# Order of one copy and one maximum on VectorE in the cross-attentions of a Perceiver block

## The chip, the core and the metric

The kernel runs on one core of a Trainium2 chip. What counts is the device time of one execution in microseconds; several runs are given by their median. Five engines work side by side and meet only at semaphores: TensorE (PE in the profile, its weight loads PEld), VectorE (DVE), ScalarE (ACT), GpSimd (POOL) and SyncE (SP), which only issues transfers.

## What is computed

Sixteen items with 64 query rows of 256 features pass through two layers. Each layer opens with a cross-attention from the 64 rows (layer-normalized) to 1601 context rows, 16 heads of 16 features. The first one adds relative-position terms to scores and values, the second one takes a mask. Cut to what matters:

```python
def cross_attention(query, context, mask, Wq, bq, Wkv, bkv, Wout, bout, num_heads):
    q = query @ Wq + bq
    kv = context @ Wkv + bkv
    k, v = (kv[0], kv[1])
    scores = jnp.einsum('bhid,bhjd->bhij', q, k) * scale
    scores = jnp.where(mask[:, None, None, :], -jnp.inf, scores)
    attn = jax.nn.softmax(scores, axis=-1)
    out = jnp.einsum('bhij,bhjd->bhid', attn, v)
    return out @ Wout + bout
...
    x = x + _L0_xattn_ref(_layernorm(x, axis=-1), ctx_1024, ctx_1024, ...)
    x = x + _L0_attn_ref(...)
    x = x + _L0_ffn_ref(...)
    x = x + _L1_xattn_ref(_layernorm(x, axis=-1), ctx_1024, mask_BxS2_bf0, ...)
    x = x + _L1_attn_ref(...)
    x = x + _L1_ffn_ref(...)
```

## The kernel before

All six stages are one program. `cross_attention` is called twice: the relative-position one (its tiles are named x0_) fills about 60 to 890 us of the span, the masked one (x3_) about 1360 to 2020 us; the latent attention and the mixture of experts lie between, the delta rule and the last feed-forward behind.

**Steps.** A cross-attention walks over its 16 items. In one step it attends to item b and works ahead on item b + 1, for which it projects keys and finds the row maxima that the softmax needs. The 1601 context rows of an item are 13 chunks of 128 (the last has 65), taken in pairs, c = 0, 2, ..., 12. The maxima are found in 16 pieces (`maximum(u)`): TensorE multiplies bf16 keys and queries into two PSUM banks (L779, 400 or 401 columns each; in the first four pieces of the relative-position attention L784 adds the relative terms), and VectorE reduces both banks in one instruction into `mx` (L634). While a step attends there is one pair of banks for this, 5 and 6, so TensorE may write piece u only when VectorE has read piece u - 1 (`max_read`).

**The order on TensorE** within a pair c is written out by hand: scores of c (L831 and L839) into banks 1 to 4; the first piece, `SCORED[c]`; the value projection of the chunks c + 2 and c + 3 (L804) into bank 0; the second piece, `PROJECTED[c]`; probabilities times values of the chunks c - 2 and c - 1 (L821) into bank 7; the third piece, `VALUED[c]`. At c = 0 there is only the second piece. In this text S4 is a piece of SCORED with number 4, P5 one of PROJECTED, V6 one of VALUED; a pair from c = 2 to c = 10 has one of each, from S1, P2, V3 to S13, P14, V15.

**VectorE** keeps its own order, also by hand. Besides the three reductions it copies the projected values from bank 0 into the tile `V` (`values(c + 2)`, L652). That copy frees bank 0 for the next value projection, and it waits for two semaphores, that of the projection and, from c = 4 on, `av_done`, which tells that TensorE is through with the old values in the slots of `V`. ScalarE takes the exponentials of the scores (L527, L529) and the projected keys (L464).

A step with both parts, attending and working ahead, runs 15 times in each cross-attention, 30 times in all. The last step of each only attends and holds no maxima.

Of the kernel before, what the change touches and what calls it, by code (L numbers as in the profile page):

```python
# [179 lines left out]
def cross_attention(nc, g, n, m, ctx_t, w, coming, x=None, rel=None, mask=None):  # L180
# [5 lines left out]
    with nc.cleanup_on_exit(), ExitStack() as ctx:  # L186
# [142 lines left out]
        PROJECTED = {0: 0, 2: 2, 4: 5, 6: 8, 8: 11, 10: 14}  # L329
# [222 lines left out]
        def _(dve):  # L552
# [31 lines left out]
            def body(bank, plan, i, p, flags):  # L584
                ahead, attend, tail = flags
# [44 lines left out]
                def maximum(u):  # L630
                    kb, k = divmod(u, 4)
                    dve.wait_ge(max_full, UN * (b + 1) + u + 1)
                    first = 5 if attend else 1 + 2 * (u % 2)
                    dve.reduce_max(mx[:, H0[k]:H0[k] + 3:2, kb], g.PS[:, first:first + 2, 0:KBS[kb]], AXX).then_inc(max_read, 1)  # L634
# [11 lines left out]
                def values(c):  # L646
                    n2 = min(2, NCH - c)
                    pb, use = plan.V[c // 2]
                    dve.wait_ge(full[pb], bank.value(pb, use))
                    if later(b) or c >= 6:  # L650
                        dve.wait_ge(av_done, NCH * b + (c - 4 if c >= 6 else 0))
                    dve.tensor_copy(V[0:CHK[c], c % 6:c % 6 + n2, :, 0:HD],  # L652
                                    PJ[pb][0:CHK[c], 0:D * n2].rearrange("p (a h d) -> p a h d", a=n2, h=H)).then_inc(free[pb], 1)
# [6 lines left out]
                for c in range(0, NCH, 2) if attend else ():  # L660
                    if ahead and c in SCORED:
                        maximum(SCORED[c])
                    if c + 2 < NCH:
                        values(c + 2)
                    if ahead and c in PROJECTED:
                        maximum(PROJECTED[c])
                    if ahead and c in VALUED:
                        maximum(VALUED[c])
                if ahead:
# [15 lines left out]
                if tail and not attend:  # L685
# [4 lines left out]
                    ln_last_vector(dve, g, n + 1)  # L690

            run(dve, body)

        @block.tensor
# [2016 lines left out]
```

## Time and profile before

| | us |
|---|---|
| median of 3 runs | 2829.75 |
| lowest and highest run | 2828.48, 2829.79 |
| span of the profiled execution | 2820.9 |
| TensorE busy with matmuls in it | 2592.8 (92%) |
| TensorE busy with weight loads | 1855.1 (66%) |
| VectorE busy | 1386.3 (49%) |
| ScalarE busy | 1042.5 (37%) |
| GpSimd busy | 532.0 (19%) |

The span runs from the first to the last instruction of one execution. It is 8.85 us shorter than the median of the runs; the time of that very execution is not listed apart. Engines overlap, so the busy times do not add up. Because each engine works through its own list in order and waits only at semaphores, what matters is not which engine is busiest but, at each place, which wait ends last.

### The profile page before, as it was taken

Reading aid. Unit: us, or ns where it says so; the run is one execution under the profiler, and the core shown is the slowest. Engines: PE = TensorE matmul, PEld = TensorE weight load, DVE = VectorE, ACT = ScalarE, POOL = GpSimd, SP = SyncE. Lnnn points to the kernel's source line nnn. Section 1 sums busy time; section 2 is a strip of 40 time slices with the busy share of each in tenths; the row PEclk is TensorE's granted clock in tenths of the full one; section 3 lists DMA queues with packets and bytes.
Section 4 is the critical chain, followed back from the end, with each engine's and each line's share of the span. In section 5 each row is a group of like instructions: output and inputs, shape, how many; then the busy total and the mean of one; then the engine's idle time right before and its main releaser. Section 6 shows DMA issues by size and latency. Waiting matters only on the chain. (4 is left out here: it accounts for less than half of the span.)

```text
span 2820.9 us, 91874 instructions
## 1 busy us (share of the span) xinstructions
PE 2592.8 (92%) x42047; PEld 1855.1 (66%) x42047; DVE 1386.3 (49%) x2238; ACT 1042.5 (37%) x1400; POOL 532.0 (19%) x400
## 2 busy tenths in 40 slices
PE   7999999999999789998999999999979999988798
PEld 3666666666666556664666666666647777777466
DVE  4454544544544831115545455555465454554378
ACT  2333333333323421114444444444434445444223
POOL 2423424434324000002111111111011111111000
PEclk8999999999998579999999999999999999999899
DMA  2110110110100030101111111112010000000200
GB/s 90 32 43 25 37 37 25 37 37 27 42 20 2 1 121 30 45 20 44 43 33 41 34 40 37 37 37 68 3 51 3 3 3 3 4 3 4 79 1 16
DMA packets 49607, 88.88 MB, mean 32 GB/s; under 512 B 8544, under 2 KB 44224, under 8 KB 47952
## 3 DMA queue, kind: packets, MB, share of 16 engines
q1 hardware_dynamic: 49200, 83.08, 9.6%
q8 instruction: 331, 5.42, 0.8%
q14 instruction: 44, 0.36, 0.0%
q0 software_dynamic: 32, 0.02, 0.0%
HBM read 82.04 MB, written 1.05 MB: 29 GB/s over the span
## 5 line engine op out<-in xcount | busy, mean ns | idle before, releaser
L634 DVE TENSOR_REDUCE x_mx<-banks 128x2 f32<-128x800 f32 (+1 forms) x512 | 505.3, 990 | 162.4 <-PE banks L779 133.2
L804 PE MATMUL banks<-x_wv,x_cT 128*128 128x256 f32 (+1 forms) x1664 | 419.3, 394 | 12.3 <-DVE x_nmb L641 12.3
L709 PE MATMUL banks<-x_cT,x_wk 128*128 128x400 f32 (+1 forms) x1024 | 385.4, 519 | 9.3 <-DMA x_cT<-in_ctx 5.9
L804 PEld LDWEIGHTS banks<-x_wv,x_cT 128*128 128x128 f32 (+1 forms) x1664 | 296.4, 187 | 83.6 <-issue 24.5
L527 ACT ACTIVATE x_PT<-banks 128x2048 f32<-128x2048 f32 (+1 forms) x112 | 196.5, 1755 | 372.1 <-PE banks L839 372.1
L529 ACT ACTIVATE x_PT<-banks,x_kbs 128x1024 f32<-128x1024 f32 (+1 forms) x208 | 221.1, 1110 | 287.7 <-PE banks L839 287.7
L652 DVE COPY x_V<-banks 128x512 f32<-128x512 f32 (+1 forms) x224 | 146.2, 653 | 338.1 <-PE banks L804 337.7
L709 PEld LDWEIGHTS banks<-x_cT,x_wk 128*128 128x128 f32 x1024 | 189.5, 193 | 140.5 <-issue 26.8
L839 PE MATMUL banks<-x_qbd,x_kT 32*128 32x128 f32 x6656 | 248.6, 272 | 0.0
L839 PEld LDWEIGHTS banks<-x_qbd,x_kT 32*128 32x128 f32 x6656 | 244.0, 183 | 3.5
L821 PE MATMUL banks<-x_PT,x_V 128*32 128x64 f32 x13312 | 233.8, 221 | 3.8 <-issue 3.0
L821 PEld LDWEIGHTS banks<-x_PT,x_V 128*32 128x32 f32 x13312 | 196.7, 110 | 55.4 <-issue 47.5
L779 PE MATMUL banks<-x_kbf,x_qbf 32*128 32x400 bf16 (+1 forms) x1024 | 174.8, 339 | 53.5 <-DVE x_mx L634 44.9
L406 POOL TENSOR_TENSOR x_kbf<-x_kT,x_mb 128x802 bf16<-128x802 f32 (+1 forms) x64 | 110.2, 1725 | 597.4 <-ACT x_kT L464 597.4
L447 POOL TENSOR_TENSOR x_Ej<-x_PT,x_kmask 128x1024 f32<-128x1024 f32 x64 | 148.7, 2358 | 128.8 <-ACT x_PT L527 128.8
L779 PEld LDWEIGHTS banks<-x_kbf,x_qbf 32*128 32x128 bf16 x1024 | 49.7, 91 | 176.2 <-DVE x_mx L634 91.8
L2069 PE MATMUL banks<-d_KQ,d_KB 64*64 64x64 f32 x3584 | 129.3, 221 | 7.4 <-ACT d_KB L1743 3.5
L1415 DVE SCALAR_TENSOR_TENSOR X<-banks,e_comb,X 128x256 f32<-128x256 f32 x72 | 34.8, 484 | 205.5 <-PE banks L1453 205.5
L464 ACT ACTIVATE x_kT<-banks,x_bk 128x400 f32<-128x400 f32 (+1 forms) x128 | 76.0, 594 | 158.6 <-PE banks L709 158.6
L2069 PEld LDWEIGHTS banks<-d_KQ,d_KB 64*64 64x64 f32 x3584 | 117.1, 134 | 23.2 <-issue 23.0
L1440 PE MATMUL banks<-XNT,e_wu 128*128 128x512 f32 x288 | 128.6, 600 | 0.4 <-DVE e_pr L1366 0.4
L1453 PE MATMUL banks<-e_wd,e_hT 128*128 128x256 f32 x576 | 127.1, 379 | 0.0
(353 smaller groups left out, 3671.4 us busy)
## 6 DMA issues: line engine op xcount, KB each, us to landing
x_cT<-in_ctx SPq DMA_DIRECT2D x96, 400.0 KB, 3.6
x_cT<-in_ctx SPq DMA_DIRECT2D x32, 401.0 KB, 3.6
e_wu<-in_mo_up SPq DMA_DIRECT2D x9, 512.0 KB, 3.5
e_wd<-in_mo_down SPq DMA_DIRECT2D x9, 512.0 KB, 4.5
x_mrow<-in_mask_row SPq DMA_DIRECT2D x1, 3202.0 KB, 16.2
t_w<-in_db_w SPq DMA_DIRECT2D x3, 1024.0 KB, 7.2
d_wqk<-in_db_qk SPq DMA_DIRECT2D x1, 2048.0 KB, 7.9
t_wgu<-in_fp_gu SPq DMA_DIRECT2D x1, 1536.0 KB, 10.4
```

The lines of the kernel that those rows point to most:

```text
L447: pool.tensor_tensor(Ej[:, j, :].rearrange("p (h q) -> p h q", h=H), PT[:, 0, 0, :].rearrange("p (h q) -> p h q", h=H), kmask[:, j, None, ...
L527: act.activation(out, got, ACT.Exp, scale=HD ** -0.5, bias=0.0).then_inc(exp_done, n2)
L529: act.activation(out[:, :, a], got[:, :, a], ACT.Exp, scale=HD ** -0.5, bias=kbs[0:CHK[c], p, c + a:c + a + 1]).then_inc(exp_done, 1)
L634: dve.reduce_max(mx[:, H0[k]:H0[k] + 3:2, kb], g.PS[:, first:first + 2, 0:KBS[kb]], AXX).then_inc(max_read, 1)
L652: dve.tensor_copy(V[0:CHK[c], c % 6:c % 6 + n2, :, 0:HD], PJ[pb][0:CHK[c], 0:D * n2].rearrange("p (a h d) -> p a h d", a=n2, h=H)).then_in ...
L709: last = pe.matmul(PJ[pb][:, 0:KBS[k]], wk[:, c, gg, :], cT[:, (p + 1) % 2, c, KB0[k]:KB0[k] + KBS[k]], start=c == 0, stop=c == KC - 1)
L779: last = pe.matmul(g.P[first + x][:, 0:KBS[kb]], qbf[rows(r), gg, :, :].rearrange("p i q -> p (i q)"), kbf[rows(r), gg, keys], start=True, ...
L804: last = pe.matmul(PJ[pb][0:CHK[c + k], D * k:D * k + D], cT[:, p, cc, 128 * (c + k):128 * (c + k) + CHK[c + k]], wv[:, cc, :], start=cc = ...
L821: last = pe.matmul(OT[r:r + 32, S * (h // 4):S * (h // 4) + S], V[0:CHK[c], c % 6, h, :], PT[0:CHK[c], c // 2 % NPT, c % 2, S * h:S * h + ...
L839: last = pe.matmul(SC[r][0:CHK[c + a], at:at + HPT * S], kT[rows(r), p, gg, 128 * (c + a):128 * (c + a) + CHK[c + a]], qbd[rows(r), p, gg, ...
L1440: last = pe.matmul(g.P[f][:, :], wu[:, q, c, 128 * f:128 * f + 128], g.XNT[:, c, 512 * t:512 * t + 512], start=c == 0, stop=c == KC - 1)
L2069: last = pe.matmul(out, lhs(E[e], hp), rhs(E[e], hp), start=k > 0 or start, stop=True, skip_group_check=True)
```

## The change

In the steps that work ahead, VectorE runs the reduction of the second piece before the copy of the values that were projected in front of it, not after it. TensorE, ScalarE, GpSimd and SyncE keep every instruction and its place.

```diff
@@ -660,10 +660,10 @@
                 for c in range(0, NCH, 2) if attend else ():
                     if ahead and c in SCORED:
                         maximum(SCORED[c])
+                    if ahead and c in PROJECTED:
+                        maximum(PROJECTED[c])
                     if c + 2 < NCH:
                         values(c + 2)
-                    if ahead and c in PROJECTED:
-                        maximum(PROJECTED[c])
                     if ahead and c in VALUED:
                         maximum(VALUED[c])
```

VectorE's list at the start of the second step of the relative-position attention, before; the first of the two copies in the first row stands ahead of the pairs, L634 is a reduction, L652 a copy:

```order
L652 COPY x0_V<-banks 128x32x16 x2
L634 TENSOR_REDUCE x0_mx<-banks 128x2 x2
L652 COPY x0_V<-banks 128x32x16
L634 TENSOR_REDUCE x0_mx<-banks 128x2 x3
L652 COPY x0_V<-banks 128x32x16
L634 TENSOR_REDUCE x0_mx<-banks 128x2 x3
```

The same place in the changed kernel:

```order
L652 COPY x0_V<-banks 128x32x16
L634 TENSOR_REDUCE x0_mx<-banks 128x2
L652 COPY x0_V<-banks 128x32x16
L634 TENSOR_REDUCE x0_mx<-banks 128x2 x2
L652 COPY x0_V<-banks 128x32x16
L634 TENSOR_REDUCE x0_mx<-banks 128x2 x3
```

Each copy in the pairs has gone behind one reduction: before, three reductions in a row are P, V and the next S; now they are V, the next S and the next P.

The end of the same step on VectorE, before:

```order
L652 COPY x0_V<-banks 128x32x16
L634 TENSOR_REDUCE x0_mx<-banks 128x2 x3
L652 COPY x0_V<-banks 65x16x16
L634 TENSOR_REDUCE x0_mx<-banks 128x2 x2
L676 TENSOR_REDUCE x0_nm<-x0_mx 128x4x2
```

And in the changed kernel:

```order
L652 COPY x0_V<-banks 128x32x16
L634 TENSOR_REDUCE x0_mx<-banks 128x2 x3
L652 COPY x0_V<-banks 65x16x16
L634 TENSOR_REDUCE x0_mx<-banks 128x2
L676 TENSOR_REDUCE x0_nm<-x0_mx 128x4x2
```

The last copy (65 rows) stands between P14 and V15, no longer in front of P14.

TensorE's list beside it, the pairs c = 4 and c = 6 of that step's kind, the same in both kernels:

```order
L779 MATMUL banks<-x0_kbf,x0_qbf 128x400 x2
L804 MATMUL banks<-x0_wv,x0_cT 128x256 x4
L779 MATMUL banks<-x0_kbf,x0_qbf 128x400 x2
L821 MATMUL banks<-x0_PT,x0_V 32x64 x32
L779 MATMUL banks<-x0_kbf,x0_qbf 128x400 x2
L831 MATMUL banks<-x0_nmb,x0_ones 128x512 x4
L839 MATMUL banks<-x0_qbd,x0_kT 128x128 x16
L779 MATMUL banks<-x0_kbf,x0_qbf 128x400 x2
```

The rows of L779 are S, P, V and the next S; nothing has moved on this engine.

## Rows read from the trace of the kernel before

**Rows 1.** Waits of the whole span: engine, line, released by: us, times, longest us.

```profile
PEld banks L779 <- DVE x_mx L634: 91.8, 278, 0.6
```

**Rows 2.** Stretch of a masked step: PE, PEld, DVE, ACT, POOL busy; clock, DMA share, GB/s.

```profile
1559.00:1588.00 29.00, 27.03 (x657) 20.17 (x655) 19.48 (x23) 14.18 (x14) 0.00 (x0) 1.00 0.17 46
```

**Rows 3.** Timeline (start, duration, instruction, idle before), masked step, P5 to P8.

```profile
1569.16 0.34 PE L779 MATMUL banks<-x_kbf,x_qbf 32*128 32x400 bf16 x2
1569.27 0.69 DVE L652 COPY x_V<-banks 128x512 f32<-128x512 f32 x1 [0.93 <-PE banks L804]
...
1569.88 0.98 DVE L634 TENSOR_REDUCE x_mx<-banks 128x2 f32<-128x800 f32 x1
1570.91 0.09 PEld L779 LDWEIGHTS banks<-x_kbf,x_qbf 32*128 32x128 bf16 x2 [0.54 <-DVE x_mx L634]
...
1571.30 0.99 DVE L634 TENSOR_REDUCE x_mx<-banks 128x2 f32<-128x800 f32 x1 [0.44 <-PE banks L779]
1572.35 0.10 PEld L779 LDWEIGHTS banks<-x_kbf,x_qbf 32*128 32x128 bf16 x2 [0.17 <-DVE x_mx L634]
...
1572.62 1.59 PEld L804 LDWEIGHTS banks<-x_wv,x_cT 128*128 128x128 f32 x8 [0.18 <-issue]
...
1574.55 0.34 PE L779 MATMUL banks<-x_kbf,x_qbf 32*128 32x400 bf16 x2
```

**Rows 4.** Timeline, the same step earlier: P2, then S4.

```profile
1563.68 0.34 PE L779 MATMUL banks<-x_kbf,x_qbf 32*128 32x401 bf16 x2
...
1566.93 0.12 PEld L779 LDWEIGHTS banks<-x_kbf,x_qbf 32*128 32x128 bf16 x2 [0.24 <-issue]
```

**Rows 5.** Timeline, the same step later: P11, S13, then P14 and V15.

```profile
1579.93 0.34 PE L779 MATMUL banks<-x_kbf,x_qbf 32*128 32x400 bf16 x2
...
1583.20 0.09 PEld L779 LDWEIGHTS banks<-x_kbf,x_qbf 32*128 32x128 bf16 x2 [0.17 <-DVE x_mx L634]
...
1583.48 1.08 PE L804 MATMUL banks<-x_wv,x_cT 128*65 128x256 f32 x4
...
1584.60 0.42 DVE L652 COPY x_V<-banks 65x256 f32<-65x256 f32 x1
1584.64 0.34 PE L779 MATMUL banks<-x_kbf,x_qbf 32*128 32x400 bf16 x2
...
1585.03 0.99 DVE L634 TENSOR_REDUCE x_mx<-banks 128x2 f32<-128x800 f32 x1
1586.07 0.09 PEld L779 LDWEIGHTS banks<-x_kbf,x_qbf 32*128 32x128 bf16 x2 [0.22 <-DVE x_mx L634]
```

**Rows 6.** Timeline, first step: two reductions in a row, then one that waits for them.

```profile
60.52 1.89 DVE L634 TENSOR_REDUCE x_mx<-banks 128x2 f32<-128x800 f32 x2 [0.27 <-PE banks L779]
...
62.44 0.19 DVE L676 TENSOR_REDUCE x_nm<-x_mx 128x8 f32<-128x32 f32 x1
```

**Rows 7.** Timeline, relative-position step, pair c = 2: P2, V3, S4.

```profile
340.75 0.30 PE L784 MATMUL banks<-x_rmaskb,x_Dxb 128*128 128x66 bf16 x4
...
341.19 0.98 DVE L634 TENSOR_REDUCE x_mx<-banks 128x2 f32<-128x802 f32 x1
...
342.51 0.30 PE L784 MATMUL banks<-x_rmaskb,x_Dxb 128*128 128x66 bf16 x4
...
342.84 1.00 DVE L634 TENSOR_REDUCE x_mx<-banks 128x2 f32<-128x802 f32 x1 [0.67 <-PE banks L784]
343.95 0.12 PEld L779 LDWEIGHTS banks<-x_kbf,x_qbf 32*128 32x128 bf16 x2
```

**Rows 8.** Timeline, relative-position step, pair c = 0: P0's last product, second value projection.

```profile
336.69 0.29 PE L784 MATMUL banks<-x_rmaskb,x_Dxb 128*128 128x66 bf16 x4
...
338.55 0.52 PEld L804 LDWEIGHTS banks<-x_wv,x_cT 128*128 128x128 f32 x3
```

**Rows 9.** Timeline, masked step, the same place: P0, second value projection.

```profile
1559.73 0.34 PE L779 MATMUL banks<-x_kbf,x_qbf 32*128 32x401 bf16 x2
...
1561.75 1.59 PEld L804 LDWEIGHTS banks<-x_wv,x_cT 128*128 128x128 f32 x8 [0.18 <-issue]
```

## The prediction, made before the changed kernel ran

> **What bounds the kernel now.** I read the waits of the whole span first. Of TensorE's waits for another engine's data inside the cross-attentions one stands out: its products for the maxima (L779) wait for VectorE's reduction L634, 91.8 us in 278 waits at the weight loads [rows 1]. Many loads had something else to wait for too, so this says where to look and not how much is to be had. The stretch of one masked step says what the engines are short of: in 29 us TensorE is busy for 27.03 and VectorE for 19.48, at a granted clock of 1.00, the upper level of 2.4 GHz, with the DMA engines at 0.17 [rows 2]. So TensorE sets the pace, VectorE has room on average, and a wait between them is worth what it costs TensorE.
>
> The timeline of one pair then shows where. P5 starts on TensorE at 1569.16. The copy starts on VectorE at 1569.27, just ahead of P5's reduction, which is ready about 0.38 after P5's start (the distance 1570.91 to 1571.30 for V6 shows it, 0.39) and starts only at 1569.88, when the copy is nearly through. V6's load, at 1570.91, follows the reduction's end (1570.86) by 0.05: TensorE stood idle 0.54 ahead of it. V6's reduction ends at 1572.29 and S7 loads at 1572.35; P8 comes 2.20 later, at 1574.55 [rows 3]. A pair therefore takes 5.39 (1574.55 - 1569.16), and two of its three pieces follow a reduction.
>
> **The change, part by part.** Nothing is added or removed; 6 copies in each of 30 steps move behind one reduction (up to 0.69 us each [rows 3]), on VectorE alone. No DMA and no other queue is touched. I count from P's start on TensorE as 0.
>
> (1) *P's reduction no longer waits for the copy.* It runs 0.38 to 1.37 (0.99 [rows 3]), and V loads at 1.43 in place of 1.75 (1570.91 - 1569.16): 0.32 earlier. TensorE can be there: from P14 to V15, where the copy stands in nobody's way already, the distance is 1.43 (1586.07 - 1584.64) [rows 5].
>
> (2) *The copy now stands before V's reduction.* That product is ready at 1.43 + 0.39 = 1.82. The unknown is when a copy can start behind a reduction, call it d after the reduction's end. The nearest rows: in P5's pair a reduction starts 0.08 before the copy's end (1569.88 against 1569.27 + 0.69 [rows 3]); two reductions in a row take 1.89, not 2 x 0.99, an overlap of 0.09, and the reduction that waits for the last of them starts 0.03 after its end [rows 6]. The row that looks like the case itself, the 65-row copy at 1584.60 right after a reduction that ends at 1584.58, does not show it: its projection on TensorE ends at 1583.48 + 1.08 = 1584.56 [rows 5], so its data was late too. I take d = -0.08, since the copy doesn't depend on the reduction, and keep d = 0.04 as the other end. With -0.08, and 0.69 for the copy, it runs 1.29 to 1.98, V's reduction 1.90 to 2.89, S loads at 2.95. Before it was 3.19 (1572.35 - 1569.16). So 0.24 of the 0.32 stays and 0.08 is given back; with d = 0.04 only 0.12 stays.
>
> (3) *Masked step.* Pairs c = 4 and 6 gain 0.24 each. Pair c = 2: P2 to S4 is 3.25 (1566.93 - 1563.68 [rows 4]); S4 opens a new block of keys, with one wait more, and came 0.12 after the reduction's end (1565.82 + 0.99), so it will be at 2.89 + 0.12 = 3.01: again 0.24. Pair c = 8: P11 to S13 is 3.27 (1583.20 - 1579.93 [rows 5]) and becomes 2.95: 0.32. Pair c = 10: P14's reduction starts at 1585.03, 0.39 after its product, since the copy of 65 rows (0.42) was over by then: nothing [rows 5]. Behind V15 the copy ends 0.39 + 0.99 - 0.08 + 0.42 = 1.72 after P14, V15's product is ready at 1.82: nothing lost. Sum 3 x 0.24 + 0.32 = 1.04.
>
> (4) *Relative-position step.* Pairs 4, 6, 8 repeat the masked rows: 0.24 + 0.24 + 0.32. In pair 2 the pieces are longer by L784. The reduction is ready 0.33 after L784's start (342.51 to 342.84), so P2's can start at 341.08, not 341.19, and V3 comes 0.10 earlier. The copy (341.99 to 342.68) is through before V3's reduction is due, at 342.74 in place of 342.84, and S4 (343.95) comes 0.10 earlier too [rows 7]. Sum 0.90.
>
> (5) *Bank 0 is held longer.* This is the price on TensorE. Before, the copy let go of the bank at 0.80, now at 1.98. The next value projection follows S by 0.27 (1572.62 - 1572.35 [rows 3]), so in the masked pairs 2 to 8 it is due at 3.22 and 1.24 are left. At c = 0, though, no V lies between. Relative-position: P0's reduction is ready at 336.69 + 0.33 = 337.02, the copy ends at 337.02 + 0.91 + 0.69 = 338.62, with 0.06 for the release 338.68, and the projection stood at 338.55 [rows 8]: 0.13 lost. Masked: 1559.73 + 0.38 + 0.91 + 0.69 + 0.06 = 1561.77 against 1561.75 [rows 9]: 0.02 lost. S1 doesn't move: the scores ahead of it end as late.
>
> A rule speaks on this place. The Trainium skill (Perfetto Trace Analysis, Matmuls) wants independent groups of matmuls to rotate through PSUM banks, so that the evacuation of one overlaps the next group. All value projections here use one bank, so by that rule holding it longer is what to avoid. The trace bears it out at c = 0 alone; in the other pairs work on other banks covers it.
>
> Sum: 15 x (1.04 - 0.02) + 15 x (0.90 - 0.13) = 26.9 us. Against the profiled execution 2820.9 - 26.9 = 2794.0 of span; what lies around the span (8.85 up to the median) stays, so 2829.75 - 26.9 = 2802.9. With x = d + 0.08 each masked step loses 5x, each relative-position step 4x (pair 2 has cover): 26.9 - 135x. At d = 0.04, x = 0.12, that is 10.7 and 2819.1. If the c = 0 loss is not there, 29.1 and 2800.7.
>
> **The rivals.** *A: the copy starts only after the reduction's end* (d from 0 to 0.04): 2819.1 at the end of it. For it: the copy waits for two semaphores. Against: both were raised well before, and waits that are met cost the copy ahead of P5 nothing that shows.
> *B: the gain is passed back* (slower side). Same mechanism, with VectorE's handover as the bound: V, S and the projection at c = 0 all stand behind the copy now. 26.9 - 135x is zero at x = 0.20 and worse than 5.7 us lost from x = 0.24 on, d = 0.16. With d = 0.22 it costs 13.6: 2843. No row shows a handover on VectorE above 0.04 without a missing product. Between x = 0.16 and 0.24 the time is unchanged, near 2830.
> *C: bank 0 decides more than I count*, the mechanism of the rule cited. If TensorE needs 0.3 more to take up the projection at c = 0 in each step, 30 x 0.3 = 9: 2811.9. The small margin at c = 0 speaks for it, the 1.24 elsewhere against.
> *D: the change does not reach the wait*, because TensorE's own products end as late as the reduction. P14 to V15 excludes it for V (1.43 there [rows 5]). For S no row tells how early the scores would let it come, only that 1.44 behind V was enough (1572.35 - 1570.91 [rows 3]); the sum puts it 1.52 behind V, so the scores don't decide.
>
> **How the numbers follow.** Forecast (d = -0.08) 0.60; A 0.18; C 0.07; unchanged 0.09; B slower 0.06. The range of 8 in 10 reaches from 2799 (no loss at c = 0, a little more overlap) to 2820 (end of A). A measurement can tell some 0.2%, 5.7 us, from nothing: the forecast, A and C (0.85) are all faster by more, 0.09 the same, 0.06 slower.
>
> **What would show it.** Right: between P5 and P8 5.15, not 5.39; L634 after P with "idle before" about 0.4, the copy directly behind it with none, 0.08 before its end; V 1.43 behind P; S behind V 1.52 instead of 1.44, with a wait for x_mx; in a relative-position step the value projection at c = 0 with a short wait for x_V L652. Masked steps shorter by about 1.0, the others by 0.8, nothing outside the cross-attentions. Wrong: the copy later than the reduction's end (A, B), or a granted clock below 1.00 in these stretches, since TensorE gets denser; neither is in the sum.

## The result, and the profile after

The changed kernel takes 2795.84 us in the median of 4 runs (2794.12 to 2798.23); beside it the kernel before took 2829.77 (4 runs, 2828.48 to 2829.99). The ratio is 0.9888 with a 95% interval of 0.9873 to 0.9904. The forecast was 2802.9 in a range of 2799 to 2820: the direction is right, the time lies below the range. The profiled execution has a span of 2795.4 and an own time (the device time of that same execution) of 2797.22.

The timeline of a masked step, P5 to P8, in the columns of [rows 3]:

```profile
1545.61 0.34 PE L779 MATMUL banks<-x_kbf,x_qbf 32*128 32x400 bf16 x2
...
1546.00 0.99 DVE L634 TENSOR_REDUCE x_mx<-banks 128x2 f32<-128x800 f32 x1 [1.21 <-PE banks L779]
1546.90 0.68 DVE L652 COPY x_V<-banks 128x512 f32<-128x512 f32 x1
1547.04 0.10 PEld L779 LDWEIGHTS banks<-x_kbf,x_qbf 32*128 32x128 bf16 x2 [0.22 <-DVE x_mx L634]
...
1547.50 0.98 DVE L634 TENSOR_REDUCE x_mx<-banks 128x2 f32<-128x800 f32 x1
...
1548.54 0.09 PEld L779 LDWEIGHTS banks<-x_kbf,x_qbf 32*128 32x128 bf16 x2 [0.23 <-DVE x_mx L634]
1548.81 1.59 PEld L804 LDWEIGHTS banks<-x_wv,x_cT 128*128 128x128 f32 x8 [0.18 <-issue]
...
1550.74 0.34 PE L779 MATMUL banks<-x_kbf,x_qbf 32*128 32x400 bf16 x2
```

P's reduction starts 0.39 after its product, not 0.72, and the weight load of V follows P by 1.43, not 1.75. The copy starts 0.09 before the reduction's end (1546.99), without idle time. V's reduction starts 0.08 before the copy's end (1547.58). S loads 2.93 behind P (3.19 before) and the pair takes 5.13 (5.39).

One step, from x_nmb to x_nmb (L641, once in each step), shows what this comes to. First a relative-position step of the kernel before and one after:

```profile
327.01 0.41 DVE L641 TENSOR_TENSOR x_nmb<-banks,x_pmask 128x256 bf16<-128x256 f32 x1
...
377.94 0.41 DVE L641 TENSOR_TENSOR x_nmb<-banks,x_pmask 128x256 bf16<-128x256 f32 x1
```

```profile
317.68 0.41 DVE L641 TENSOR_TENSOR x_nmb<-banks,x_pmask 128x256 bf16<-128x256 f32 x1
...
367.80 0.41 DVE L641 TENSOR_TENSOR x_nmb<-banks,x_pmask 128x256 bf16<-128x256 f32 x1
```

50.93 became 50.12, 0.81 less. A masked step, before and after:

```profile
1552.11 0.42 DVE L641 TENSOR_TENSOR x_nmb<-banks,x_pmask 128x256 bf16<-128x256 f32 x1 [0.78 <-PE banks L873]
...
1597.90 0.42 DVE L641 TENSOR_TENSOR x_nmb<-banks,x_pmask 128x256 bf16<-128x256 f32 x1 [0.83 <-PE banks L873]
```

```profile
1528.81 0.42 DVE L641 TENSOR_TENSOR x_nmb<-banks,x_pmask 128x256 bf16<-128x256 f32 x1 [0.78 <-PE banks L873]
...
1573.51 0.42 DVE L641 TENSOR_TENSOR x_nmb<-banks,x_pmask 128x256 bf16<-128x256 f32 x1 [0.83 <-PE banks L873]
```

45.79 became 44.70, 1.09 less. 15 x 0.81 + 15 x 1.09 = 28.5 us. Between the two recorded spans lie 25.5, between the first medians 33.9. What makes the difference to 28.5 is the first question for the experiments.

### The profile page after: what moved, and what is told of

Same layout as the page of the kernel before. It is cut to its first block and busy times, and to the rows that moved or that the text cites. A ratio compares the mean times of both kernels' runs of the same rounds, so it can differ in the third digit from the quotient of the medians.

```text
span 2795.4 us, 91874 instructions
## 1 busy us (share of the span) xinstructions
PE 2591.0 (93%) x42047; PEld 1854.2 (66%) x42047; DVE 1373.8 (49%) x2238; ACT 1042.6 (37%) x1400; POOL 532.3 (19%) x400
## 5 line engine op out<-in xcount | busy, mean ns | idle before, releaser
L634 DVE TENSOR_REDUCE x_mx<-banks 128x2 f32<-128x800 f32 (+1 forms) x512 | 506.1, 991 | 361.6 <-PE banks L779 248.4
L804 PE MATMUL banks<-x_wv,x_cT 128*128 128x256 f32 (+1 forms) x1664 | 420.5, 395 | 14.1 <-DVE x_nmb L641 12.3
L804 PEld LDWEIGHTS banks<-x_wv,x_cT 128*128 128x128 f32 (+1 forms) x1664 | 296.9, 188 | 89.6 <-issue 21.9
L652 DVE COPY x_V<-banks 128x512 f32<-128x512 f32 (+1 forms) x224 | 144.2, 644 | 121.4 <-PE banks L804 121.4
L779 PE MATMUL banks<-x_kbf,x_qbf 32*128 32x400 bf16 (+1 forms) x1024 | 174.2, 338 | 22.4 <-DVE x_mx L634 3.8
L779 PEld LDWEIGHTS banks<-x_kbf,x_qbf 32*128 32x128 bf16 x1024 | 49.8, 91 | 142.0 <-issue 72.2
```

The source lines that it names most:

```text
L652: dve.tensor_copy(V[0:CHK[c], c % 6:c % 6 + n2, :, 0:HD], PJ[pb][0:CHK[c], 0:D * n2].rearrange("p (a h d) -> p a h d", a=n2, h=H)).then_in ...
L779: last = pe.matmul(g.P[first + x][:, 0:KBS[kb]], qbf[rows(r), gg, :, :].rearrange("p i q -> p (i q)"), kbf[rows(r), gg, keys], start=True, ...
L804: last = pe.matmul(PJ[pb][0:CHK[c + k], D * k:D * k + D], cT[:, p, cc, 128 * (c + k):128 * (c + k) + CHK[c + k]], wv[:, cc, :], start=cc = ...
```

## The experiments

Single executions of these kernels differ by several us. So besides the ratio to the kernel before, taken in the same session, I use the length of a step in each trace. Every second step has a length that repeats to 0.02 us, and that is the one given below. The steps between are longer and less even, in the kernel before most often 52.67 and 47.51, in the changed one 51.85 and 46.43: 0.82 and 1.08 less, so the gain is the same in them.

**The kernel before, unchanged**

> The kernel before, unchanged, for its spread. The profiled execution before had a span of 2820.9 and the median of the runs was 2829.75. Theory 1 (the change acts inside the cross-attentions alone, and the rest of the 33.9 us between the medians is what one execution differs from another): the executions of this kernel have spans between about 2820 and 2829, each about 2 us under its own time, with the pairs P5 to P8 at 5.39 in all of them. Theory 2 (the change also shortens something outside the cross-attentions): all spans near 2821, and 8.85 us lie around the span in each.

Measured: 2824.96 (12 runs, 2817.30 to 2831.45), and 2824.73 (17 runs, 2818.46 to 2836.04) for the runs beside it. All 29 own times are 1.75 to 2.90 us above the span of the same execution. So theory 2 is out: the 8.85 us that I had put around the span are not there. Theory 1 holds, though the spans reach further than it said, from 2815.5 to 2834.2. By this gap the first profiled execution (2820.9) took about 2823, an estimate, 7 us less than the runs that its median was made of. The step lengths are 50.92 and 45.78.

**The changed kernel, unchanged**

> The changed kernel, unchanged. Its profiled span was 2795.4, its steps 50.12 (relative-position) and 44.70 (masked) where they were 50.93 and 45.79, which makes 28.5 in 30 steps. Theory 1: the same steps again, and a ratio to the kernel before of 0.988 to 0.990, with stages outside that shift by up to 5 us either way. Theory 2: the same stages outside the cross-attentions are shorter again, by about 5 in sum.

Measured: 2796.99 (5 runs, 2791.05 to 2798.42), ratio 0.9892 (0.9874 to 0.9911), steps 50.12 and 44.70. The stages of all six recorded executions of the two kernels, in us, cut at starts of L641 (the fourth stage begins with the second masked step, since the third is cut behind the first one). The masked attention lies earlier than the 1360 to 2020 us of the section on the kernel before: there its first step starts at 1317.7 and its last at 2014.5.

| | up to first L641 | 15 relative steps | between, with 1 masked step | 14 masked steps | rest | span |
|---|---|---|---|---|---|---|
| before | 66.9 | 772.6 | 525.7 | 649.4 | 806.4 | 2820.9 |
| before, second | 61.8 | 773.0 | 525.5 | 649.8 | 809.5 | 2819.5 |
| before, third | 61.2 | 773.1 | 522.8 | 649.6 | 806.2 | 2812.9 |
| after | 61.9 | 760.4 | 523.3 | 634.7 | 815.1 | 2795.4 |
| after, second | 60.9 | 760.4 | 523.6 | 634.7 | 811.6 | 2791.2 |
| after, third | 62.2 | 760.5 | 523.3 | 634.0 | 809.2 | 2789.2 |

The two columns with the steps repeat within 0.8 us for one kernel and part by 12.1 to 12.7 and 14.6 to 15.8 between the two. The other three vary by 3 to 9 us: the start of the first recording of before was 5 us longer than the others, the rest of the first of after 9 us longer than the shortest. The last stage leans one way: 806.2, 806.4 and 809.5 before, 809.2 to 815.1 after, and 809.5 to 815.7 in the five variants below. No instruction of that stage was changed, and the medians of many runs show no such loss (their differences are 27.7 and 29.8 in the second and third session, beside the 28.5 of the steps), so whether this is chance is not shown.

What happened at that start: the first stretch of before, of after, and of the variant with the change in the relative-position attention alone, whose start was the shortest of all (columns of [rows 2]):

```profile
0.00:66.80 66.80, 50.12 (x176) 25.40 (x176) 28.72 (x60) 15.47 (x26) 14.14 (x19) 0.87 0.30 95
```

```profile
0.00:61.90 61.90, 46.79 (x176) 23.70 (x176) 28.74 (x61) 15.47 (x26) 14.22 (x19) 0.94 0.32 103
0.00:58.70 58.70, 44.05 (x176) 22.91 (x176) 28.73 (x60) 15.48 (x26) 14.17 (x19) 1.00 0.34 108
```

The same 176 matmuls, with a mean granted clock of 0.87, 0.94 and 1.00: the upper level of 2.4 GHz all the time in the shortest, the lower of 1.2 GHz for a part of the others, the longest part in before. Engines other than TensorE are busy for the same time. In the cross-attentions the mean is 1.00 in both kernels. Over the 17 runs beside the second recording, own time and mean clock go against each other (correlation -0.79; between -0.46 and -0.81 in the other sets of 12 or 17 runs of before). That goes together, and alone shows no cause.

**One attention at a time**

```diff
-                    if ahead and c in PROJECTED:
+                    if ahead and c in PROJECTED and mask:
                         maximum(PROJECTED[c])
                     if c + 2 < NCH:
                         values(c + 2)
+                    if ahead and c in PROJECTED and not mask:
+                        maximum(PROJECTED[c])
```

> The reduction goes before the copy in the masked attention alone. Theory 1 (local and additive): masked steps 44.70, relative-position steps 50.93, 15 x 1.09 = 16.4 us less than before in the steps, 2813 +- 3. Theory 2 (a gain outside that comes with the change): more than 16.4 here and in the other half both, or all of the surplus in one of the two.

Measured: 2808.31 (6 runs), ratio 0.9935 (0.9917 to 0.9953), 16.4 less than the 2824.73 beside it. Steps 50.94 and 44.71.

The other half has `mask` and `not mask` exchanged.

> The reduction goes before the copy in the relative-position attention alone. Theory 1: relative-position steps 50.12, masked steps 45.79, 15 x 0.81 = 12.2 us less than before in the steps, 2817 +- 3. Theory 2: the surplus of about 5 us over the steps shows here, since every stage behind this attention is shifted.

Measured: 2809.67 (6 runs), ratio 0.9941 (0.9922 to 0.9960), 15.1 less. Steps 50.12 and 45.79. In the steps each half has its own gain and none of the other's. The times agree with 16.4 and 12.2 within their intervals (2824.73 x 0.0018, about 5 us either way), which also means that they could not show a gain of some 3 us outside. The stages of the relative-position half show none: 524.9 between and 812.1 behind, no shorter than in the kernel before. Both times lie outside my ranges, 5 and 7 us below my 2813 and 2817, which had been counted from 2829.75: a further sign that this level was high.

**The copy one reduction further back**

```diff
                     if ahead and c in PROJECTED:
                         maximum(PROJECTED[c])
-                    if c + 2 < NCH:
-                        values(c + 2)
                     if ahead and c in VALUED:
                         maximum(VALUED[c])
+                    if c + 2 < NCH:
+                        values(c + 2)
```

> VectorE's copy goes one reduction further back, behind the third piece of a pair (V). Theory 1 (V's reduction is held by the copy, and bank 0 becomes the bound once the copy is late enough): V's reduction starts when its product is ready (1.81 behind P, now 1.89), S gains about 0.06, but the copy ends at about 3.40 behind P while the next value projection is due at 3.12, so the projection waits 0.3 for x_V L652 and the pair P5 to P8 is 5.3 to 5.4, not 5.13: about 1.1 us a step lost in each attention, about 2829 +- 4 us on the scale on which the kernel before has 2825 to 2830 and the changed one 2797. Rival (bank 0 has cover anyway, VectorE's last reduction alone sets the pace): 0.06 a pair better than the changed kernel, about 2790.

Measured: 2820.87 (12 runs) against 2822.84 (17 runs), ratio 0.9987 (0.9977 to 0.9997). Nearly the whole gain is gone. A masked step takes 45.56, a relative-position step 51.03: 0.86 and 0.91 more than in the changed kernel (1.1 expected). Against the kernel before the steps make 15 x 0.10 - 15 x 0.23 = -1.95 us, the medians -1.97. The 2829 +- 4 that I had expected is missed by 8, for it had the high level in it and 1.1 a step. The timeline of the masked step, P5 to P8:

```profile
1562.90 0.34 PE L779 MATMUL banks<-x_kbf,x_qbf 32*128 32x400 bf16 x2
...
1564.71 0.99 DVE L634 TENSOR_REDUCE x_mx<-banks 128x2 f32<-128x800 f32 x1 [0.44 <-PE banks L779]
...
1565.62 0.68 DVE L652 COPY x_V<-banks 128x512 f32<-128x512 f32 x1
1565.76 0.09 PEld L779 LDWEIGHTS banks<-x_kbf,x_qbf 32*128 32x128 bf16 x2 [0.17 <-DVE x_mx L634]
...
1566.36 1.99 PE L804 MATMUL banks<-x_wv,x_cT 128*128 128x256 f32 x8 [0.25 <-DVE x_V L652]
1568.28 0.10 PEld L779 LDWEIGHTS banks<-x_kbf,x_qbf 32*128 32x128 bf16 x2 [0.33 <-issue]
```

V's reduction now starts as soon as its product is there (1.81 behind P), S comes at 2.86. But the value projection that follows S by 0.27 elsewhere follows it by 0.60, for bank 0 is held till 1566.30: the pair takes 5.38 (1568.28 - 1562.90). TensorE's waits of that whole execution show it in one row:

```profile
PE banks L804 <- DVE x_V L652: 27.4, 120, 0.3
```

The 120 are 4 pairs in each of 30 steps. So bank 0 is the bound as soon as the copy is one reduction later.

**The old order at c = 0 alone**

```diff
-                    if ahead and c in PROJECTED:
+                    if ahead and c in PROJECTED and c:
                         maximum(PROJECTED[c])
                     if c + 2 < NCH:
                         values(c + 2)
+                    if ahead and c in PROJECTED and not c:
+                        maximum(PROJECTED[c])
```

> The changed kernel with the old order at c = 0 alone. Theory 1 (the change costs the relative-position step 0.13 at c = 0, since the second value projection waits for the copy to release bank 0): relative-position steps 0.13 shorter, 49.99 for 50.12, masked steps 44.70 as they are, 2 us in sum, which the times may not tell but the traces do. Rival (the 0.13 are not bank 0): steps unchanged.

Measured: relative-position steps 50.00 for 50.12, masked steps 44.70. The 0.12 come back where they were predicted. The changed kernel at this place, P0's last product, the copy, and the second value projection:

```profile
327.36 0.30 PE L784 MATMUL banks<-x_rmaskb,x_Dxb 128*128 128x66 bf16 x4
...
328.60 0.68 DVE L652 COPY x_V<-banks 128x512 f32<-128x512 f32 x1
...
329.33 0.51 PEld L804 LDWEIGHTS banks<-x_wv,x_cT 128*128 128x128 f32 x3
```

The load of L804 comes 0.05 behind the copy's end (329.28), 1.97 behind L784; before it was 1.86 [rows 8]. In time the variant has 2792.29 (6 runs), ratio 0.9891 (0.9873 to 0.9909): 15 x 0.12 = 1.8 us is too little for the times to tell.

**The copies on ScalarE**

Behind its exponentials of a pair, ScalarE takes over `values(c + 2)`; VectorE keeps the copy ahead of the pairs.

```diff
                             act.activation(out[:, :, a], got[:, :, a], ACT.Exp, scale=HD ** -0.5,
                                            bias=kbs[0:CHK[c], p, c + a:c + a + 1]).then_inc(exp_done, 1)
+                        if c + 2 < NCH:
+                            cv = c + 2
+                            nv = min(2, NCH - cv)
+                            pb, use = plan.V[cv // 2]
+                            act.wait_ge(full[pb], bank.value(pb, use))
+                            if later(b) or cv >= 6:
+                                act.wait_ge(av_done, NCH * b + (cv - 4 if cv >= 6 else 0))
+                            act.activation(V[0:CHK[cv], cv % 6:cv % 6 + nv, :, 0:HD],
+                                           PJ[pb][0:CHK[cv], 0:D * nv].rearrange("p (a h d) -> p a h d", a=nv, h=H),
+                                           ACT.Copy).then_inc(free[pb], 1)
...
-                    if c + 2 < NCH:
-                        values(c + 2)
```

> The copies of the projected values inside the pairs go to ScalarE, behind its exponentials; VectorE keeps only the first copy of a step. Theory 1 (what is left of the copy's price is V's reduction started 0.08 late, and bank 0 at c = 0): V's reduction starts 1.81 behind P, S 2.86 or as early as the scores allow, the pair P5 to P8 5.06, and relative-position steps gain 0.13 more at c = 0: about 0.3 us a masked step and 0.35 us a relative-position step, 9 us in sum, 2788 where the changed kernel has 2797. Rival (ScalarE is late for the next exponentials, or S is held by TensorE's scores): the pair stays at 5.13 or grows.

Measured: 2785.06 (4 runs, 2783.44 to 2788.36), ratio 0.9863 (0.9840 to 0.9886). Steps 49.79 and 44.34, so 0.33 and 0.36 less than in the changed kernel, 10.4 us in 30 steps. Its masked pair, where L787 is the product called L779 elsewhere, L644 the reduction and L538 the copy:

```profile
1539.56 0.34 PE L787 MATMUL banks<-x_kbf,x_qbf 32*128 32x400 bf16 x2
1539.66 0.60 ACT L538 ACTIVATE x_V<-banks 128x512 f32<-128x512 f32 x1 [0.15 <-PE banks L812]
...
1541.37 0.99 DVE L644 TENSOR_REDUCE x_mx<-banks 128x2 f32<-128x800 f32 x1 [0.44 <-PE banks L787]
1542.42 0.09 PEld L787 LDWEIGHTS banks<-x_kbf,x_qbf 32*128 32x128 bf16 x2 [0.17 <-DVE x_mx L644]
...
1544.62 0.34 PE L787 MATMUL banks<-x_kbf,x_qbf 32*128 32x400 bf16 x2
```

V's reduction starts 1.81 behind P, S loads at 2.86, the pair takes 5.06, all as expected of theory 1. This version beats both kernels in its steps. In its times it lies below too, though the changed kernel itself did not run in that session: its slowest run is 2788.36, the fastest of the 14 runs of the changed kernel 2789.68.

Theory 1 had given the relative-position step more (0.35) than the masked one (0.3), and it came out the other way. The reason stands at c = 0. There the masked step of before had S1 wait for P0's reduction:

```profile
1561.48 0.10 PEld L779 LDWEIGHTS banks<-x_kbf,x_qbf 32*128 32x128 bf16 x2 [0.18 <-DVE x_mx L634]
```

In the changed kernel that reduction is over early, S1 loads 1.48 behind P0 in place of 1.75, and the second value projection stands waiting for bank 0:

```profile
1536.43 0.34 PE L779 MATMUL banks<-x_kbf,x_qbf 32*128 32x401 bf16 x2
...
1537.73 0.68 DVE L652 COPY x_V<-banks 128x512 f32<-128x512 f32 x1
1537.91 0.10 PEld L779 LDWEIGHTS banks<-x_kbf,x_qbf 32*128 32x128 bf16 x2
...
1538.46 1.59 PEld L804 LDWEIGHTS banks<-x_wv,x_cT 128*128 128x128 f32 x8 [0.45 <-DVE x_V L652]
...
1540.39 0.34 PE L779 MATMUL banks<-x_kbf,x_qbf 32*128 32x401 bf16 x2
```

With the copy on ScalarE the projection doesn't wait there:

```profile
1530.61 0.34 PE L787 MATMUL banks<-x_kbf,x_qbf 32*128 32x401 bf16 x2
...
1534.39 0.34 PE L787 MATMUL banks<-x_kbf,x_qbf 32*128 32x401 bf16 x2
```

P2 follows P0 by 3.78, by 3.96 in the changed kernel and by 3.95 before (1563.68 - 1559.73). In the relative-position step it is 3.97, 4.18 and 4.06. So 0.18 of the 0.36 and 0.21 of the 0.33 are got at c = 0, where bank 0 bound the changed kernel in both attentions; the rest comes in pairs, 0.06 or 0.07 in each.

**Both kernels once more**

> The kernel before once more, in another session, for the level. So far its single runs lay between 2814.5 and 2836.0 with medians of 2829.8 (4 runs), 2824.7 (17) and 2822.8 (17). Theory 1 (the first 4 runs, all within 1.5 us of each other, were a draw from the upper half of that spread): a median near 2824 again. Theory 2 (a chip can have its own level): the whole session lies near 2829 or higher, and the changed kernel with it.

> The changed kernel beside it. Theory 1: 2796 +- 3, 28 less than the kernel before in the same session, as the 30 steps say (15 x 0.81 + 15 x 1.09 = 28.5). Theory 2: about 34 less, as between the medians of the first session.

Measured: 2821.42 (12 runs) and 2820.76 (17 runs) for the kernel before, 2790.98 (5 runs, 2789.68 to 2797.15) for the changed one, ratio 0.9900 (0.9885 to 0.9914). With 2829.8 the first session remains alone at the top. The difference of medians was 33.9, 27.7 and 29.8 in the three sessions, and 28.5 in the steps. The changed kernel came out below the 2796 +- 3 that I had expected; the difference of 29.8 lies near the 28 of theory 1 and not near 34. So theory 1 holds for the gain. That the first four runs were a mere draw is not borne out: of the 75 later runs of the kernel before only 10 reach 2828.48, so by this share four out of four is a matter of some 3 in 10,000 (an estimate that takes runs as independent). Nor was it a level that both kernels shared, for the changed one had 2795.84 in that session, between its later 2790.98 and 2796.99. What lifted those four runs stays open.

## Why the prediction was wrong, point by point

**The wait and its place: right.** P's reduction stood behind the copy and V behind that reduction. (1) had V at 1.43 behind P: measured 1.43.

**The part that is given back: right.** (2) took a copy to start 0.08 before a reduction's end (measured 0.09), V's reduction at 1.90 (1.89) and S at 2.95 (2.93). Rival A is thereby out, and B with it: the handover came out below nothing, not above 0.16. The copy on ScalarE confirms from the other side what VectorE's copy still costs V's reduction: 1.81 in place of 1.89. The granted clock of the steps stayed at 1.00.

**The sums of a step: nearly right.** (3) and (5) gave 1.02 for the masked step, measured 1.09; (4) and (5) gave 0.77 for the other, measured 0.81. Each pair gained 0.01 to 0.03 more than its term, since the copy took 0.68 and started 0.01 earlier. In all 28.5 for 26.9.

**Bank 0 at c = 0: right as a loss against before, wrong beside it.** 0.13 predicted for the relative-position step, 0.12 shown by undoing it; 0.02 for the masked one, about 0.01 measured. But (5) also said "S1 doesn't move: the scores ahead of it end as late". S1 did move, from 1.75 to 1.48 behind P0 in the masked step, since it had waited for P0's reduction, and the wait for bank 0 swallowed it. So without the wait for bank 0 P2 could come 0.17 earlier than before in a masked step and 0.09 in the other, a gain that the sum had at nothing; only the copy on ScalarE got it. Rival C had a slower takeup of the projection; it was 0.05 behind the copy's end. Its mechanism is real, though, and the copy one reduction further back shows how near it is: there the 1.24 us of cover are used up.

**D** was out: both V and S moved.

**The step that failed** is the one from the span to the time: "what lies around the span (8.85 up to the median) stays". I subtracted the gain of one execution from the median of others, and called the difference a fixed cost around the span. Every listed execution has 1.74 to 3.01 there. The profiled execution was thus about 7 us faster than the three runs of the median, and these three, though within 1.3 us of each other, lay high among the later ones, which reach from 2814.5 to 2836.0 with medians of 2820.8 to 2825.0. Made against the profiled execution's own time the sum would have been 2820.9 + 2 - 26.9 = 2796.0, beside a measured 2795.8; so close a match is partly luck, as the spread shows. And the range, built from mechanisms alone, had no term for this spread, up to 17.6 us from the lowest to the highest of a set of 12 or 17 runs. Of the 7.1 us between forecast and result 1.6 are the mis-sized gain (26.9 for 28.5), and 5.4 are this level; why it was high in the first session stays open.

## What to carry to other kernels

On an engine that works in order, put the instruction whose result the bottleneck waits for ahead of one whose result has slack, and count both ends of the slack: here the copy could go back by one reduction (28.5 us gained), not by two (nearly all lost), because the bank that it frees is the next bound. If another engine has room between its own duties, try to move the work there: here, with ScalarE busy for 37% of the span, that was better than every order tried on VectorE. Look, too, at what a wait behind the one removed will swallow: a wait that is gone at one place (S1) came back at the next (bank 0). And make the forecast against the own time of the execution that was profiled, with a range that holds the spread of single executions.

## What the runs showed of the hardware

A VectorE instruction can start before the shown end of the one ahead of it: 0.09 us from reduction to copy (1546.90 against 1546.99), 0.08 from copy to reduction, in the pairs where the next one's data was ready; TensorE, which waits for the semaphore, came 0.05 after the shown end. The Trainium skill (Perfetto Trace Analysis, Per-engine timelines) explains the sign: the shown end is the acknowledgement of the writes, while the next instruction may begin to fetch once execution is over. That section gives no size for it.

The same kernel on the same chip had own times 17.6 us apart (2818.46 to 2836.04 in 17 runs). In the recorded executions, whose spans differ by up to 8 us for one kernel, the differences lie outside the steps of the cross-attentions. At the start they go with the clock: 66.8 us at 0.87, 61.9 us at 0.94 and 58.7 us at 1.00 for the same 176 matmuls, which were busy for 50.12, 46.79 and 44.05 us. For the last stage, 806.2 to 815.1 us, the mean clock was 0.97 in the recordings of 806.2, 806.4 and 815.1 alike, and what makes it long stays open.
